# Layer 0 of a four-layer graph network: which engine writes zeros over a range that has been stored, and in how many pieces

## The reference

```python
def _L0_gnn_ref(x, edge_row, edge_col, edge_val, W):   # called with (x, src, dst, edge_weight, L0_gnn_W)
    msgs = edge_val[:, None] * x[edge_col]
    agg = jax.ops.segment_sum(msgs, edge_row, num_segments=N_NODES)
    return agg @ W.T
x = _layernorm(x + _L0_gnn_ref(x, src, dst, edge_weight, L0_gnn_W), axis=-1)
```

## Time and profile before

| | |
|---|---|
| median of 3 runs | 3432.19 us (3420.75 to 3432.79) |
| profiled execution: its own time / its span | 3436.49 / 3435.2 us |
| busy over the span | PE 2842.3, PEld 2102.1, DVE 1980.4, ACT 1166.3, POOL 2504.0 us |
| mean granted TensorE clock | 0.911 of full |

### The profile page before, as it was taken

One profiled execution on the slowest core, in us unless ns is written; L12 is line 12 of the kernel. 1 busy time (PEld: TensorE's weight loads), 2 busy tenths in 40 slices (PEclk: granted clock), 3 DMA queues, 4 the chain that ended last, 5 costly groups with the idle time before them and its releaser, 6 DMA issues. The chain is left out here.

```text
span 3435.2 us, 60104 instructions
## 1 busy us (share of the span) xinstructions
PE 2842.3 (83%) x19220; PEld 2102.1 (61%) x19220; DVE 1980.4 (58%) x6384; ACT 1166.3 (34%) x3693; POOL 2504.0 (73%) x2238
## 2 busy tenths in 40 slices
PE   5989888778888769789968987678888875699995
PEld 4877666557777658444447774366666674466664
DVE  7888988877787538442253344433444564244557
ACT  5555665566777548100010003400111232001123
POOL 3888888887887666577747777777777774777773
PEclk9999999999999879899969997589999997799997
DMA  8777888888999789778847876755566554988884
GB/s 274 114 138 110 151 157 159 154 151 187 188 187 182 162 221 310 195 210 236 237 112 193 229 222 176 230 155 156 167 178 180 161 174 129 293 234 250 249 252 138
DMA packets 658435, 652.78 MB, mean 190 GB/s; under 512 B 87902, under 2 KB 606476, under 8 KB 656588
## 3 DMA queue, kind: packets, MB, share of 16 engines
q0 software_dynamic: 153600, 258.41, 37.3%
q1 hardware_dynamic: 430670, 331.83, 31.4%
q10 hardware_dynamic: 73854, 58.70, 5.5%
HBM read 434.19 MB, written 214.52 MB: 189 GB/s over the span
## 5 line engine op out<-in xcount | busy, mean ns | idle before, releaser
L1700 POOL DMA_INDIRECT A<-rows_buf,big x572 | 943.1, 1649 | 267.5 <-issue 144.1
L886 POOL DMA_INDIRECT rows_buf<-T,idx x888 | 849.1, 956 | 276.0 <-issue 271.4
L980 PE MATMUL PSA<-S,rows_buf 128*128 128x128 bf16 (+2 forms) x5904 | 585.7, 254 | 214.0 <-DMA rows_buf<-X,idx 102.7
L980 PEld LDWEIGHTS PSA<-S,rows_buf 128*128 128x128 bf16 (+2 forms) x5904 | 524.3, 142 | 296.8 <-DMA rows_buf<-X,idx 89.5
L886 POOL DMA_INDIRECT rows_buf<-X,idx x528 | 509.2, 964 | 160.9 <-issue 155.7
L1036 DVE TENSOR_TENSOR accT<-PSA,accT 128x256 f32 (+2 forms) x354 | 132.6, 375 | 838.2 <-PE PSA L980 832.6
L1387 PE MATMUL PSA<-XRS,rows_buf 128*128 128x256 f32 x1144 | 313.4, 398 | 4.0 <-DMA XRS<-in_xpad 3.8
L1553 DVE TENSOR_TENSOR accT<-PSA,accT 128x392 f32 (+5 forms) x366 | 239.6, 655 | 109.0 <-PE PSA L1484 52.3
L1399 ACT ACTIVATE rows_buf<-PSA 128x512 f32<-128x512 f32 x286 | 168.1, 594 | 227.5 <-PE PSA L1387 186.3
L797 ACT ACTIVATE accT<-accT,vec 128x500 f32<-128x500 f32 (+3 forms) x26 | 17.7, 693 | 667.7 <-DVE accT L795 667.6
L1387 PEld LDWEIGHTS PSA<-XRS,rows_buf 128*128 128x128 f32 x1144 | 210.2, 197 | 31.2 <-issue 6.4
(11 more groups left out here) (318 smaller groups left out, 5655.8 us busy)
## 6 DMA issues: line engine op xcount, KB each, us to landing
XRS<-Ad SPq DMA_DIRECT2D x400, 256.0 KB
Ad<-accT SPq DMA_DIRECT2D x224, 196.0 KB, 3.4
XRS<-in_xpad SPq DMA_DIRECT2D x192, 128.0 KB, 5.0
Awd<-accT SPq DMA_DIRECT2D x48, 392.0 KB, 3.5
A<-accT SPq DMA_DIRECT2D x9, 1600.0 KB
rows_buf<-T,idx POOLq DMA_INDIRECT x888
rows_buf<-A SPq DMA_DIRECT2D x24, 512.0 KB
accT<-A SPq DMA_DIRECT2D x24, 512.0 KB, 6.3
```

What stands on the lines that cost most here:

```text
L886: s_hg[slot(i)][j // 2].on(pool.indirect_dma_start(Gv(slot(i), j), None, table, bass.IndirectOffsetOnAxis(idx[:, c:c + 1], 0)), 16)
L980: last = pe.matmul(PS[bank_of(i)][0:F, W * h:W * h + W], Gv(slot(i), j)[:, o:o + F], hits[:, i % SRING, j, :], start=j + part == 0, stop=j ...
L1700: s_k[n].on(pool.indirect_dma_start(A, bass.IndirectOffsetOnAxis(tgt[:, c:c + 1], 0), G[:, i % RING, j, :], None, compute_op=ALU.add), 16)
```

## The change

Both VectorE clears go. ScalarE writes zeros instead, reading the one-column tensor `nought` broadcast along the row. Aww (6272 32-bit columns) is written in two pieces of 3136. A cold range's Aw (6272 16-bit columns) is addressed as 3136 32-bit words and written in two pieces of 1568. The first piece stands at the end of step final+3 in ScalarE's list and waits for the first four stored parts; the second stands at the end of final+4 and waits for all eight. Only the second raises `s_azw` or `s_azc`. The check of the hot ranges (L1569) stays. No zero is summed or compared by the new instructions.

```diff
-        def clear_weights(w):
-
-            v.wait_ge(s_aww, 16 * PARTS * (w + 1))
-            part = Aww.bitcast(I32)
-            v.tensor_scalar(part, part, 0, None, ALU.bitwise_and).then_inc(s_azw, 1)
-
-        def clear_counts(w):
-
-            v.wait_ge(s_aw[TURN[w] % 2], 16 * PARTS * (TURN[w] // 2 + 1))
-            part = Aw[buffer_of(w)]
-            v.tensor_scalar(part, part, 0.0, None, ALU.mult).then_inc(s_azc, 1)
+        def clear_weights(w, k):
+
+            sc.wait_ge(s_aww, 16 * (PARTS * w + 4 * k + 4))
+            done = sc.activation(Aww[:, 3136 * k:3136 * k + 3136], nought[:, 0:1].broadcast_to([128, 3136]), ACT.Identity)
+            if k:
+                done.then_inc(s_azw, 1)
+
+        def clear_counts(w, k):
+
+            sc.wait_ge(s_aw[TURN[w] % 2], 16 * (PARTS * (TURN[w] // 2) + 4 * k + 4))
+            part = Aw[buffer_of(w)].bitcast(F32)[:, 1568 * k:1568 * k + 1568]
+            done = sc.activation(part, nought[:, 0:1].broadcast_to([128, 1568]), ACT.Identity)
+            if k:
+                done.then_inc(s_azc, 1)
...
                     if i == cleared_at(w, k):
                         window_clear(w, k)
+                        if k % 2:
+                            clear_weights(w, k // 2)
+            for w in CLEARED:
+                for k in range(2):
+                    if i == cleared_at(w, 2 * k):
+                        clear_counts(w, k)
...
-            for w in range(HWIN):
-                if i == cleared_at(w, 2):
-                    clear_weights(w)
-            for w in CLEARED:
-                if i == cleared_at(w, 2):
-                    clear_counts(w)
```

## The result

| | before | after |
|---|---|---|
| median of 9 runs each, same chip | 3429.77 us (3420.75 to 3436.16) | 3440.66 us (3433.35 to 3451.00) |
| profiled execution: its own time / its span | 3436.49 / 3435.2 us | 3441.03 / 3439.8 us |
| busy over the span: DVE, ACT, POOL | 1980.4, 1166.3, 2504.0 us | 1938.9, 1247.4, 2459.7 us |

The ratio after to before is 1.0031, with a 95% interval of 1.0019 to 1.0044: the change costs about 11 us. The forecast was 3434 us, range 3404 to 3462, and the likeliest outcome a difference within 0.5%. So the total came out as forecast, on the slower side of it.

What follows compares the result with a forecast made beforehand. POOL was late up to about 760 us, then the front: ACT with PE from 800, SP's stores from 1060. Terms -18+17-6-5+16-4+0 sum to 0, forecast 3434 us, own range 3419 to 3449, widened to 3404 to 3462.

Steps and rivals of the forecast that it cites:

- POOL's stretches: POOL's scatters beside VectorE's 25 clears in layer 0: all 39.3 us of stretching taken as gone.
- (a): POOL's stalls: relief at the full ring before 800 us gains the front 18 us; after 800 us nothing.
- (c): Cold clears of six ranges before 800 us: ACT has slack, VectorE is relieved; 5 us gained.
- (b): Six hot clears moved to ACT: one piece of two charged, 17 us lost; VectorE's relief, 6 us gained.
- the hot share of (a): Hot clears' part of the 18 us in (a); six hot clears hold 16.3 us of stretches.
- (d): Cold clears from 800 to 1060 us: 18 ACT pieces at 0.9 us, 16 us lost; VectorE 4 us gained.
- (e): Four cold clears after 1060 us: SP's stores set the pace; 0 taken, ends 0 and 9.3 us lost.
- The signs: Listed trace marks: scatters to about 2.1 us, pieces 2.8 and 1.5, POOL's waits up 20 to 40, end near 1244.
- the full ring: ACT's waits for POOL at the ring of four steps: under 15 us instead of 35.
- rival B: ACT becomes the bound between steps 92 and 122 and at hot clears: 28 us slower, 3460 us; chance 0.24.
- Rival A: POOL sets the time, front before 800 us has slack: 24 us gained, 3408 us (3393 with all stretches); chance 0.19.
- Rival C: SP's stores set layer 0 from 800 us on and hide gains and losses: 3432 us; chance 0.12.

Runs made afterwards that it cites:

- cold_only: Kernel before, but ScalarE clears the counts of the 19 cold ranges (38 pieces); VectorE keeps the six hot clears; ratio 0.9984 to before.
- hot_only: Kernel before, but ScalarE clears Aww of the six hot ranges (12 pieces); VectorE keeps the 19 cold clears; ratio 1.0031 to before.
- after_again: The changed kernel run once more, no edit; ratio 1.0046 to before.
- early_cold_only: Kernel before, but ScalarE writes the counts of cold ranges 6 to 10 (ten pieces); all other clears stay on VectorE; ratio 0.9997 to before.
- last_hot_dve: The changed kernel, but VectorE clears the last hot range's weight matrix in one instruction as before; ratio 1.0034 to before.
- no_clears: Kernel before with 24 of 25 VectorE clears cut to two columns; only the last hot range's stays whole; ratio 0.9973 to before.
- late_double: The changed kernel with each cold piece from range 11 on written twice by ScalarE (28 pieces more); ratio 1.0167 to before, 3482.81 us.
- before_again: The kernel before run once more, unchanged, for a second trace; ratio 1.0009.
- all_dve_two_pieces: Kernel before, but VectorE makes all 25 clears in two halves a step apart, ScalarE writes none; ratio 0.9982 to before.

## Why the prediction was right in total and wrong in parts

The working clock is the table above. Of before and of after I take the mean of two traces; single traces of one kernel differ by 2 to 5 us, and smaller terms than that can't be told.

**POOL's stretches, their size: right.** 39.3 us forecast, 42 us seen, and the paired clears were the cause: in cold_only, where the hot clears stay on VectorE, the longest scatter is 4.78 us; in hot_only, with only cold clears there, it is 3.27 us. The rule of the Trainium skill, SBUF — State Buffer, "Who interferes with whom" (ScalarE doesn't hold the port pair that VectorE and GpSimd share), agrees with the trace: the longest of 86 scatters beside ACT's zeros lasts 1.76 us in after and 1.79 in after_again. The line's longest, 2.19 us, stands at 45.16 us, before any clear. What the rule doesn't say is what the 42 us are worth, and they were worth little.

**Terms (a) and (c), the cold part: right.** By the prediction's shares the early cold ranges bring 5 us for VectorE's relief and about 6 of the 18 us of (a) (their part of the 23.9 us of stretches is 23.9 - 16.3 = 7.6). Step 91 comes at 741.0 (cold_only) and 740.5 us (early_cold_only) against 751.0 us before: 10 us forecast as 11, the two terms together; no run parts them. (The 23.9 us leave out the clear of range 11 at 795 us, 0.6 us; nothing hangs on it.)

**Term (b), the hot clears: this step failed, by 9 to 15 us.** The prediction charged one piece of two, 17 us, less 6 for VectorE and less the hot share of (a), about 12: a gain of 1 us. Measured at step 91, hot_only is 7.5 us later than before, and the changed kernel (755.0) 14 us later than cold_only. Two assumptions on the cost were behind it. One was that ACT's 140 us of waits for PE would take up a part: they stayed at 146.3 us. Those waits lie in other places of the list than the burst of checks and zeros, in which ACT has no gap, and slack elsewhere is not slack here. The other was the delay of the checks alone. In the five hot clears before 760 us VectorE's two kinds of waits (L1553 for the checks, L1563 for the zeros) grew from 3.3 + 4.4 to 36.2 + 10.6 us, by 39.1; its clears there had taken 5 x 3.43 = 17.1. VectorE's 5.5 us of waits for stored parts ahead of these clears (L1577) went too. That leaves 16.5 us, 3.3 us a clear instead of 2.8 - 1. The step clock agrees: the five stretches of five steps listed under last_hot_dve are 15.5 us longer in sum. At the second hot clear, steps 40 to 43 take 29.9 and 30.8 us (hot_only 30.0) against 25.0 and 23.9 before. The remaining steps up to 91 are 12 us shorter, about what the cold part brings.

The gain was set too high as well. no_clears has none of the five hot clears before step 91 at full width, on either engine, and gets there at 733.1 us, 8 us ahead of cold_only, which has them on VectorE. For these five the prediction had a gain of 10 us from the hot share of (a) and 5 us for VectorE's relief. With a gain of 8 us, ACT's hot pieces cost 15 us (from hot_only) to 22 us (from the changed kernel), forecast as 14. Single traces leave 2 to 5 us of doubt on each.

**Term (d), the cold pieces from 800 to 1060 us: mechanism right, size too high.** 16 us less 4 were forecast. From step 96 to 128, which hold 20 of ACT's pieces, the busy times (PE, PEld, DVE, ACT, POOL), the granted clock, the share of DMA and its GB/s were, in before, after, after_again and late_double:

```profile
805.99:1076.48 270.49, 241.35 (x1646) 196.71 (x1645) 212.69 (x549) 199.21 (x662) 217.82 (x132) 0.99 0.91 187
```

```profile
813.09:1085.05 271.96, 240.43 (x1651) 196.03 (x1650) 196.80 (x539) 225.15 (x683) 201.69 (x130) 1.00 0.90 185
```

```profile
816.83:1088.42 271.59, 240.97 (x1650) 195.99 (x1649) 196.97 (x538) 224.75 (x683) 202.59 (x130) 1.00 0.90 185
```

```profile
817.27:1128.47 311.20, 252.26 (x1650) 202.21 (x1649) 198.34 (x539) 255.19 (x703) 203.08 (x131) 0.97 0.81 164
```

ACT has 26 us more work, and the stretch gets 1.5 us longer than in before and 4.7 us shorter than in before_again (276.3 us). Over all kernels, those that clear late ranges whole on VectorE take 270.5, 276.3, 265.9, 265.4 and 265.1 us (mean 268.6), those with ACT's pieces once 271.9, 271.6, 276.1, 274.8, 271.3 and 271.3 us (mean 272.8). That is 4 us, less than two traces of before differ, and no_clears, which writes almost nothing, takes 268.4, and all_dve_two_pieces, with halves on VectorE, 271.2. So the term was between nothing and 4 us. The mis-sized number is the 0.9 us a piece. I had let one wait of about 1 us absorb part of one piece in each pair; the row of 28.2 us in 29 waits was a pool that took in 17 us. late_double shows where this ends: a second piece costs at least its whole length.

**Term (e), the tail: right as far as it goes.** From step 128 to the last scatter before takes 154.5 and 149.1 us, after 148.7 and 150.1. DVE's wait for stored parts became waits of the first addition for the zeros, and ACT itself waited under 1 us for parts. From 1060 to 1190 us of the changed kernel:

```profile
DVE accT L1553 <- ACT accT L1584: 9.4, 2, 5.6
...
ACT accT L1584 <- DMA Ad<-accT: 0.9, 1, 0.9
```

By stretch, the mean of after less that of before is +4 us up to step 91 (forecast: -12), +6 from 91 to 96 (forecast: nothing there), -2 from 96 to 128 (forecast: +12) and -2 behind it. So (b) was too low by about as much as (d) was too high, and that the sum of zero came near the truth (6 us in layer 0) is partly luck.

**The signs.** The pieces' lengths, the full ring (6.6 us), the scatters (only two over 2.1 us) and the end of the layer came as listed, and ACT's waits for stored parts stayed under 1 us. POOL's waits for ACT rose by 55 us, more than the 20 to 40. DVE L1553 waits at the clears, which was rival B's sign.

**Rival A (POOL sets the time)** fell twice: the changed kernel lost POOL's stretches and got slower, and no_clears gained 10 us, not 24 to 39. **Rival B (ACT becomes the bound)** was nearer than the forecast at the hot clears: its full price there, 34 us less VectorE's 6 and the hot share 12 of (a), is a loss of 16 us for six clears, 13 for the five before step 91, against the 7.5 and 14 measured there. For the cold pieces it failed. Its own test, ACT's busy share in that stretch reaching 84%, came in (215.5 of 260 is 83%), and PE's wait for ACT rose from 12.5 to 19.7 us; but its condition, that the waits don't shrink, did not hold. In late_double, one piece further on, it does. **Rival C (SP's stores hide all)** falls too: layer 0's end follows the pieces from 1209.5 to 1280.3 us.

**What the split shows.** Taking 24 of the clears away is worth 10 us, and cutting all of them in two about 7. In halves a step apart the longest scatter falls from 4.54 us (4.75 in before_again) to 3.10 us in all_dve_two_pieces, and POOL's line gets 13 to 16 us shorter in sum. Whether the shorter stretch each, the smaller sum, or the earlier first half is the reason, no run separates.

**Left open.** Layer 0 ends 6 us later after the change, the medians differ by 11. Over all kernels the gains of layer 0 come through only in part: 20 us become 10 in no_clears, 10 us become 1 in early_cold_only. The layers behind start at another phase, and the granted clock from 1245 to 1400 us was 0.92 in one trace of before and 0.89 in one of after, but no run here separates that. Two traces of one kernel differ by 0.02 themselves: 0.92 and 0.94 for before, 0.89 and 0.91 for after.

The 6 us from step 91 to 96 (60.0 us in after, 53.8 before) are open in part. The traces show the chain there. TensorE's first block of the dense product waits for SP's loads of Awd (L1266), in before and in after:

```profile
777.13 1.11 PE L1594 MATMUL PSA<-ident,accT 128*128 128x128 f32 x4 [7.90 <-DMA accT<-Awd]
```

```profile
784.60 1.11 PE L1597 MATMUL PSA<-ident,accT 128*128 128x128 f32 x4 [8.44 <-DMA accT<-Awd]
```

These loads stand in SP's list behind four stores of counts, and these wait for the additions behind the last hot clear (760.29 in before, 768.28 in after). So the addition, the stores (761.60, 769.59), the loads (772.37, 779.78) and the product all come 7 to 8 us later, although step 91 is equally early in these two traces. In last_hot_dve (60.4 us) the addition is no earlier, since VectorE's clear waits for stored parts and ends at 769.3. So ACT's zeros for this range are not the cause alone. What makes the stored parts late is open: cold_only (58.3 us) and no_clears (57.9 us) have no hot zeros on ACT and are nearly as slow there.

## What to carry to other kernels

A stretched instruction on one engine is worth what the engine that is late can gain; look for who waits at both ends of the ring before adding up stretches. Slack counts only where it stands in the list: short waits right behind the new piece took in nearly all of 26 us of new work, and 140 us of waits elsewhere in the list did not shrink for five bursts of 5.6 us. A pool of slack is used up: a second piece in the same place cost at least its length. Where a long operation disturbs its neighbours, try cutting it in two, with the halves a step apart, before moving it to another engine; here the cut was worth 0.2% and the whole move cost 0.3 to 0.5%.

## What the runs showed of the hardware

A clear in 32-bit columns and one in 16-bit columns both stretch the scatter beside them, and so does a half clear: 1.78 us on VectorE with a scatter of 2.89 us. The scatter is stretched whichever of the two starts first: of the 25 stretched scatters of before, 16 end 0.07 to 0.12 us after the clear beside them, the one at 367.23 among them, which had started 1.02 us before its clear, and the other 9 end 1.40 to 1.43 us after it. In the two traces of after no scatter beside ACT's writes of zeros lasts over 1.8 us. These writes cost 2.81 us for 3136 and 1.50 us for 1568 words, 0.83 ns a word and 0.19 us beside. The second piece of late_double, over the same words, took 1.508 us. And the same program took 3430 us on one chip and 3783 on another, with layer 0 equally long (last scatter at 1231.0 and 1228.9 us) and a mean granted clock of 0.911 and 0.888.
